# Maxima of the unmasked cross attentions as three one-pass products of high and low parts

## The reference, cut to what matters

```
q = split_heads(LN(x) @ Wq + bq)      # 16 heads of 16
k = split_heads(ctx @ Wk + bk);  v = split_heads(ctx @ Wv + bv)
logits = q @ k^T / 4                  # + mask in layers 1 and 3
out = softmax(logits) @ v;  x = x + out @ Wo + bo
```

## Time and profile before

| | |
|---|---|
| median of 3 runs | 4879.96 us (4879.55 to 4884.21) |
| profiled execution, its time | 4880.05 us |
| profiled execution, its span | 4878.3 us (1.75 us lie outside) |
| layer 0's cross attention | 29.5 to 763 us |
| layer 2's cross attention | 2859 to 3587 us |
| PE busy over the span | 4319.7 us (89%) |
| L591, all four layers | 4096 records, 457.8 us |
| DVE, ACT, POOL busy | 2473.7, 1964.9, 553.3 us |

### The profile page before, as it was taken

How to read it: one execution, slowest core, us unless ns; L and a number is a source line. 1 busy time by engine, 2 the same in 40 slices (tenths; PEclk the granted TensorE clock), 3 DMA queues, 4 the chain that set the end, 5 groups by cost and what they waited for, 6 DMA issues and landing times. The chain is left out here.

```text
span 4878.3 us, 144357 instructions
## 1 busy us (share of the span) xinstructions
PE 4319.7 (89%) x65736; PEld 3428.9 (70%) x65736; DVE 2473.7 (51%) x4177; ACT 1964.9 (40%) x3848; POOL 553.3 (11%) x262
## 2 busy tenths in 40 slices
PE   7999996599999979999986789999962789999968
PEld 5877774488888858888853568777741668888844
DVE  4555553566666655545545445555525255555530
ACT  3554442233333334444432335455431244444421
POOL 1111111000000011111112011111102011111100
PEclk9999997599999989999988799999975899999989
DMA  2111100021111121111022011111012611111000
GB/s 69 43 36 43 36 23 16 24 77 49 49 49 49 39 63 37 37 44 37 31 54 53 19 52 43 36 43 36 30 25 84 224 57 38 41 40 38 24 20 19
DMA packets 89472, 223.14 MB, mean 46 GB/s; under 512 B 28736, under 2 KB 52307, under 8 KB 86147
## 3 DMA queue, kind: packets, MB, share of 16 engines
q1 hardware_dynamic: 85360, 209.06, 13.6%
q10 hardware_dynamic: 2736, 2.75, 0.2%
q0 software_dynamic: 768, 2.10, 0.1%
HBM read 196.16 MB, written 9.32 MB: 42 GB/s over the span
## 5 line engine op out<-in xcount | busy, mean ns | idle before, releaser
L690 DVE TENSOR_REDUCE x_pm<-banks 128x4 f32<-128x1536 f32 (+2 forms) x512 | 935.5, 1827 | 687.2 <-PE banks L591 687.2
L792 ACT ACTIVATE x_pl<-banks 128x384 f32<-128x384 f32 x1536 | 628.8, 498 | 710.1 <-PE banks L574 710.1
L516 POOL TENSOR_TENSOR x_cl<-xnT,x_ch 128x1601 fp32r<-128x1601 f32 x116 | 386.4, 3331 | 2171.9 <-ACT x_ch L807 2171.9
L797 ACT ACTIVATE x_kT<-banks,x_bk 128x384 f32<-128x384 f32 (+2 forms) x512 | 305.1, 596 | 530.9 <-PE banks L602 530.9
L614 PE MATMUL banks<-x_wh,x_ch 128*128 128x256 f32 (+1 forms) x1664 | 489.6, 294 | 0.0
L574 PE MATMUL banks<-x_q,x_kT 32*128 32x128 f32 x13312 | 481.8, 276 | 3.1 <-issue 3.0
L591 PE MATMUL banks<-x_kT,x_q 32*128 32x384 f32 (+2 forms) x4096 | 457.8, 512 | 14.0 <-DVE x_v L722 9.0
L614 PE MATMUL banks<-x_wh,x_cl 128*128 128x256 f32 (+1 forms) x1664 | 468.4, 281 | 0.0
L614 PE MATMUL banks<-x_wl,x_ch 128*128 128x256 f32 (+1 forms) x1664 | 467.0, 281 | 0.0
L602 PE MATMUL banks<-x_ch,x_wh 128*128 128x384 f32 (+2 forms) x1024 | 410.3, 401 | 43.7 <-DVE x_cl L773 43.1
L574 PEld LDWEIGHTS banks<-x_q,x_kT 32*128 32x128 f32 x13312 | 435.7, 184 | 6.9 <-issue 4.3
(11 more groups left out here) (339 smaller groups left out, 7010.5 us busy)
## 6 DMA issues: line engine op xcount, KB each, us to landing
xnT<-in_ctxT SPq DMA_DIRECT2D x120, 800.5 KB, 4.3
e_w<-in_L_pack SPq DMA_DIRECT2D x91, 384.0 KB, 3.1
e_w<-in_L_pack SPq DMA_DIRECT2D x21, 1154.0 KB, 7.8
a_swap<-a_raw SPq DMA_DIRECT2D x64, 128.0 KB, 2.3
actT<-in_ctxT SPq DMA_DIRECT2D x8, 800.5 KB, 4.9
e_rw<-routed_rows SPq DMA_DIRECT2D x64, 64.0 KB, 2.8
x_rows<-e_zero SPq DMA_DIRECT2D x1, 2688.0 KB, 9.6
e_xt<-x_rows ACTq DMA_DIRECT2D x3, 896.0 KB, 10.5
```

Source lines behind the costliest of these rows:

```text
L516: nc.gpsimd.tensor_tensor(cl[:, u, k, 0:CTX], staged(b, k), ch[:, u, k, 0:CTX], ALU.subtract).then_inc(low_done, 1)
L690: nc.vector.tensor_reduce(pm[:, c, :, g], src[:, :, 0:hi - lo], AX.X, ALU.max).then_inc(max_done, 1)
L792: nc.scalar.activation(probabilities(c, j, lo, hi).rearrange("p t q -> p (t q)"), mine[j][:, 0:(hi - lo) * P], ACT.Exp).then_inc(exp_done, 1)
L797: nc.scalar.activation(kT[:, c, lo:hi], mine[1 if g == 0 and inside(b if c else b - 1) else 0][:, 0:hi - lo], ACT.Identity, bias=col[:, c: ...
```

## The change

In the unmasked layers L591's products are made of parts. `qh` is the query rounded to F32R, `ql` the rest; `kh` and `kl` the same of the keys, in a ring of four units. Three F32R products (qh kh, ql kh, qh kl) for each of the four row groups are summed in the bank: 12 matmuls in place of 4 float32 ones. The masked layers keep theirs. The width of the last group becomes even (322), with a zero column.

- ACT: after each eviction L797 it waits for it and copies the unit from `kT` into `kh`.
- POOL: `keys_low` subtracts `kh` from `kT` into `kl`, one operation for each unit, between the `split_low` ones, whose place moves to g2 of each half.
- DVE: `take_q` gets a copy (`qh`) and a subtraction (`ql`), each behind a wait; before the loop `take_q` is called twice, and two small memsets of the ring's pad column are added.
- PE: before the maxima of each unit two more waits, for `q_low` and `k_low`. Scores and everything else are as before, with `kT` and `qb`.

```diff
@@ pool @@
+            def keys_low(unit):
+                c, g = unit // 4 % KC, unit % 4
+                lo, hi = KEYS[g]
+                s = unit % RING
+                pool.wait_ge(k_high, unit + 1)
+                nc.gpsimd.tensor_tensor(kl[:, s, 0:hi - lo], kT[:, c, lo:hi], kh[:, s, 0:hi - lo], ALU.subtract).then_inc(k_low, 1)
+
             pool.wait_ge(low_done, 2)
-            for k in range(KC):
-                split_low(1, 1, k)
-            for b in range(2, B):
-                for k in range(KC):
-                    split_low(b, b % 2, k)
+            for b in range(-1, B - 1):
+                for c in range(KC):
+                    for g in range(4):
+                        if not masked:
+                            keys_low(CYCLES * (b + 1) + 4 * c + g)
+                        if g == 2 and inside(b + 2):
+                            split_low(b + 2, b % 2, c)
@@ maxima @@
+                else:
+                    unit = CYCLES * b + 4 * c + g
+                    pe.wait_ge(q_low, b + 1)
+                    pe.wait_ge(k_low, unit + 1)
+                    even = hi - lo + (hi - lo) % 2
+                    for n, (y, z) in enumerate(((qh, kh), (ql, kh), (qh, kl))):
+                        for j in range(4):
+                            r = slice(32 * j, 32 * j + 32)
+                            last = nc.tensor.matmul(into[j][:, 0:even], y[r, u, c], z[r, unit % RING, 0:even], start=(n == 0),
+                                                    stop=(n == 2))
@@ take_q @@
+                if not masked:
+                    dve.wait_ge(q_staged, 2 * b + 2)
+                    nc.vector.tensor_copy(qh[:, u], qb[:, u]).then_inc(q_high, 1)
+                    dve.wait_ge(q_high, b + 1)
+                    nc.vector.tensor_tensor(ql[:, u], qb[:, u], qh[:, u], ALU.subtract).then_inc(q_low, 1)
@@ scalar, after the eviction of the keys @@
+                            if not masked:
+                                unit = k + CYCLES
+                                act.wait_ge(k_taken, unit + 1)
+                                if unit >= RING:
+                                    act.wait_ge(m_full, unit - RING + 1)
+                                nc.scalar.activation(kh[:, unit % RING, 0:hi - lo], kT[:, c, lo:hi], ACT.Copy).then_inc(k_high, 1)
```

More of the change, by code:

```diff
@@ L393, in cross_attention @@
     EARLY = GROUPS[0][1]
+    RING = 4
+    LAST = KEYS[3][1] - KEYS[3][0]
     names = ("wv_in bias_in raw_in0 raw_in1 wk_high wk_low wv_high wv_low high_done low_done pad_set mask_in0 mask_in1 side_set shift_set "
-             "sums_set q_staged m_full max_done z_step z_ready z_turned nm_ready s_full exp_done k_full k_taken v_full "
+             "sums_set q_staged q_high q_low k_high k_low m_full max_done z_step z_ready z_turned nm_ready s_full exp_done k_full k_taken v_full "
              "v_taken pv_full o_taken den_full inverted out_ready")
@@ L398, in cross_attention @@
             block, wv_in, bias_in, raw_in0, raw_in1, wk_high, wk_low, wv_high, wv_low, high_done, low_done, pad_set, mask_in0, mask_in1,
-            side_set, shift_set, sums_set, q_staged, m_full, max_done, z_step, z_ready, z_turned, nm_ready, s_full,
+            side_set, shift_set, sums_set, q_staged, q_high, q_low, k_high, k_low, m_full, max_done, z_step, z_ready, z_turned, nm_ready, s_full,
             exp_done, k_full, k_taken, v_full, v_taken, pv_full, o_taken, den_full, inverted, out_ready):
@@ L412, in cross_attention @@
         qb = net.sb(tag + "_q", [P, 2, KC, P], ctx=mem)
+        if not masked:
+            qh = net.sb(tag + "_qh", [P, 2, KC, P], F32R, ctx=mem)
+            ql = net.sb(tag + "_ql", [P, 2, KC, P], F32R, ctx=mem)
+            kh = net.sb(tag + "_kh", [P, RING, HALF], F32R, ctx=mem)
+            kl = net.sb(tag + "_kl", [P, RING, HALF], F32R, ctx=mem)
         side = net.sb(tag + "_side", [P, 2, PADDED], F32R, ctx=mem) if masked else None
@@ L588, in maxima @@
                         nc.tensor.matmul(into[j][:, 0:even - lo], ones_r[r], side[r, u, lo:even], start=True, stop=True)
[L589 to L592, removed]
+                    for j in range(4):
+                        r = slice(32 * j, 32 * j + 32)
+                        last = nc.tensor.matmul(into[j][:, 0:hi - lo], qb[r, u, c], kT[r, c, lo:hi], start=False, stop=True,
+                                                skip_group_check=True)
+                else:
[4 more added lines that the diff above has]
+                    for n, (y, z) in enumerate(((qh, kh), (ql, kh), (qh, kl))):
+                        for j in range(4):
+                            r = slice(32 * j, 32 * j + 32)
+                            last = nc.tensor.matmul(into[j][:, 0:even], y[r, u, c], z[r, unit % RING, 0:even], start=(n == 0),
+                                                    stop=(n == 2))
                 last.then_inc(m_full, 1)
@@ L678, in _ @@
             pe.wait_ge(wk_low, 1)
-            pe.wait_ge(pad_set, 2)
+            pe.wait_ge(pad_set, 2 if masked else 4)
             pe.wait_ge(shift_set, 2 + masked)
@@ L766, in _ @@
             nc.vector.memset(cl[:, :, :, CTX:EVEN].bitcast(F32), 0.0).then_inc(pad_set, 1)
+            if not masked:
+                nc.vector.memset(kh[:, :, LAST:LAST + 1].bitcast(F32), 0.0).then_inc(pad_set, 1)
+                nc.vector.memset(kl[:, :, LAST:LAST + 1].bitcast(F32), 0.0).then_inc(pad_set, 1)
             take_q(0, 0)
@@ L815, in _ @@
             act.wait_ge(bias_in, 32)
+            if not masked:
+                act.wait_ge(pad_set, 4)
             each_batch(one)
```

## The result

The changed kernel takes 4889.93 us (median of 20 runs) against 4880.39 for the kernel before (20 runs): a ratio of 1.0016, 95% interval 1.0009 to 1.0024. It is slower by about 8 us by the ratio, 9.5 by the medians; I had forecast 4875.1 and a gain of 4.9. The time lies in the range, the sign is wrong. All ratios here leave out the single disturbed run, one of e14 (13851.42 us, at a granted clock of 0.268).

The account below looks back on a forecast made before the run. PE was taken to set the pace, with gains limited by ACT's exponentials. Thirty full batches (7.8 us) and some 13 other units (0.9), less 3.8 for the openings, gain 4.9: 4880.05 becomes 4875.1, range 4864 to 4893.

Parts of the forecast that it names:

- POOL. ... Cost 0: POOL's four added subtractions a half, below 5 us in 21 us, fit beside split_low and cost nothing.
- rival 4: A queue behind PE (ACT's nm or POOL) becomes the bound: 3 to 6 us, 4878 to 4881; 0.52 together with the forecast.
- w: Cost of PE's two more waits between scores and maxima, where the last semaphore is late: 0.08 us, between 0 and 0.22.
- rival 2: PE's two added waits before the maxima cost 0.11 us each and replace the gain: slower, 4890 to 4895, chance 0.16.
- take_q on DVE: In c0g0 the added copy (0.35 us) and subtraction (0.43) let L690 start at about 333.62, 0.08 later than before.
- Swallowing c0g1's gain: DVE's later take_q delays divide and take_v, so c0g1 and c0g2 together gain only 0.05 - w.
- The floors of ACT: Key projection starts no sooner than 0.54 us after the exponentials: gain 0 in g0 and c1g1, 0.03 in c1g2.
- The gain of a unit: Maxima take three passes for four, saving 0.21 us at 512 wide, 0.16 at 384, 0.13 at 321.
- Rival 3: Two of three maxima rounds wait for their weights, so a unit is 0.21 us longer than forecast: about 4905, chance 0.04.
- the rule that stands beside rival 3: From the Trainium skill: on PE a weight load overlaps with matmuls in flight only where the row group differs.
- The sum over a batch: Gain of a full batch in the unmasked layers: (0.05 - w) + (0.21 - w) + 0.03 + (0.21 - w) = 0.26 us.
- The opening: Before the loop, two take_q calls with four added DVE operations delay PE's first matmul: 1.9 us a stage, 3.8 in all.

Follow-up runs that it names:

- e14: Changed kernel with keys_low of c0g1 behind the division, q_low wait once per maxima turn, opening take_q later, context loads after attend in all layers: 4804.11 us, ratio 0.9846.
- e1: Changed kernel, but in c0g1 POOL starts keys_low only after DVE's division of the batch: 4863.67 us, ratio 0.9981.
- e9: Changed kernel, but the reciprocal is written back to its PSUM bank and the multiply reads it there, POOL's order unchanged: 4861.87 us, ratio 0.9980.
- e8: e1's kernel with only the product qh kh made, ql kh and qh kl left out: 4834.02 us, ratio 0.9909 to the kernel before.
- e13: Kernel before with two more long-satisfied PE waits in front of each maxima unit of the unmasked layers: 4885.31 us, ratio 1.0010.
- e2: e1's kernel with PE's wait for q_low kept only at one unit of eight: 4845.05 us, ratio 0.9941 to the kernel before.
- e5: Kernel before with one extra 768-wide POOL subtraction, result unused, in each c0g1 of the unmasked layers: 4888.63 us, ratio 1.0038.

## Why the prediction was wrong

**The step that failed** is "POOL. ... Cost 0", and with it the price in rival 4, "POOL holding DVE's take_q ... 0.1 to 0.2 us a batch". I asked only whether POOL had time and whether kl was due in time. I did not set POOL's new start beside DVE's operations at that moment. The numbers were there: keys evicted at 335.35, a copy of 0.5, so a start at about 335.95, over an operation of 1.0; and the multiply of the division at 336.19 in the kernel before. I had even written that `divide` to `take_v` has no slack. What the runs show in its place: POOL's subtraction holds the multiply for 0.94 us in place of 0.29. c0g2 grew by 0.47, and with e1's edit it stands at 4.40, so the clash costs 0.6 a batch, 17 us over the 28 batches that have it. Without it the ratio is 0.9981, which is 9 us of gain; on that, the forecast of 4.9 would have had the sign.

That the time lies in the range is luck. Its upper part was priced for w = 0.22, and rival 2 (slower, 4890 to 4895) has the right number by the wrong cause: e1 and e9 keep both waits and are faster than the kernel before.

**take_q on DVE** was right in size: L716 of c0g1 begins right behind the subtraction, 0.83 us after `take_q`'s two old operations end (333.23 to 334.06), which is what I had (332.79 to 333.62). Swallowing c0g1's gain was half right: in e1 c0g1 and c0g2 together gain 0.06, I had -0.03.

**The floors of ACT** held to 0.02 us: in g0 attend starts no earlier, c1g1 gained nothing, c1g2 0.03. e8 shows the same for two passes more.

**The gain of a unit** was a little too large. From the maxima to the key projection the medians fell from 0.86 to 0.73, from 1.07 to 0.90 and from 0.75 to between 0.65 and 0.67 us, which is 0.13, 0.17 and some 0.09 where I had 0.16, 0.21 and 0.13. Rival 3 is refuted all the same: four F32R matmuls follow the four before on the same row groups after 0.18 us (333.46, 333.64), as single ones of 384 columns do in L628 (334.22, 334.40), and the weights of the second four are being loaded (333.29) while the first four stream. So the rule that stands beside rival 3 does not hold in these rows.

**w** was 0.08 for each late cycle; e13 shows 0.21 in c0g1 and -0.05 to 0.06 in the others. The medians from the first scores matmul to the first maxima one tell more. c0g1 takes 1.27 us before, 1.38 in e2 with one wait more, 1.49 in e13 with two: 0.11 for each. The four that follow `take_v` take 1.01 with no wait beyond the common ones (c1g2 and c1g3 before), 1.12 with one (c0g2 and c0g3 before), and 1.07 or 1.08 with two or three. So my 0.11 for one and 0.06 for a pair were both right readings, but c0g2 and c0g3 had one already and gained 0.05 by getting more. c0g3 and c1g3 gained 0.22 and 0.10 where I had 0.13 each. The sum over a batch, 0.26, is 0.41 in e1.

**Attend was not in the sum.** Its stops over 0.25 us are 18.0 us of the kernel before's unmasked layers. The change moved them: layer 2's c0g0 +7.0 us, layer 0's -5.6. Their total stayed, 18.5 us, so they did not cost it the sign, but that was chance: in e2 they are 6.0 us. I had seen batches of 42.6 and of 46.4 us in one layer and took only the plain one. They had to be in the range, and as a rival.

**The opening**: 1.6 us a layer against 1.9, in size and place as said.

## What to carry to other kernels

Before an operation is given to an engine with room, lay its start beside what the neighbours do then, and look for DVE operations with two SBUF operands under a POOL subtraction; here one semaphore (e1) or one operand in PSUM (e9) avoided the clash. A pass saved on a busy PE counts only up to the next engine's release: price it cycle by cycle. Where plain batches and slow ones alternate, find out first what separates them: here a load issued 7 us later, behind attend and not ahead of it, was worth more than the whole change. And where PE stops for nothing that the profile names, look at the times of the queue that it calls instruction.

## What the runs showed of the hardware that I had not expected

- A DVE TENSOR_TENSOR with both inputs in SBUF took 0.94 us in place of 0.29 when POOL had begun a subtraction 0.2 us earlier, and ended 0.15 us after it (in e5 too, where POOL was 0.7 us ahead); with one input in PSUM it took 0.29 us under the same POOL operation. DVE's reduction (2.29 us) and `take_v` (0.76), which read PSUM, take the same time beside POOL as without it.
- PE's instructions came in packets of 16 KB, 256 records each, mostly of 0.9 to 1.4 us. In streams of short matmuls (64 columns, 208 to a half) PE stopped for 0.3 to 2.3 us at the border of a packet, in all 488 stops found. Most of them (27 of 38 in the kernel before) ended within 8 us of the issue of a context load of 800 KB. Moving the loads of the loop behind attend, 54 in two layers, took 28 us off the kernel before; moving those of all four took 58.
- Two waits that had long been satisfied, before a group of matmuls, cost 0.21 us in one cycle and between -0.05 and 0.06 in the others; where the start hangs on `take_v`, one cost 0.11 and two or three 0.06. I have no reason for that.
